# In the 128-row tiles of a mixture-of-experts FFN, layer 1 takes the high and low halves of the rows side by side, and VectorE adds the two halves of each PSUM bank

## The chip, the cores and the metric

The kernel runs on one core of one Trainium2 chip. Its time is the device time of one execution in microseconds (us). Three executions of the kernel before took 754.45, 755.43 and 755.51 us, so their median is 755.43 us. Besides these, one execution was recorded by the hardware profiler.

## The reference, cut to what matters

A block over x of shape (4, 1024, 256), that is 4096 tokens of 256 numbers. The first half is a gated linear recurrence with a residual. The second half is the mixture of experts that this change is about: each token goes to the two of eight experts that score highest.

```
x = x + ga * attn(layernorm(x) * (1 + ca) + sa)
h = layernorm(x) * (1 + cb) + sb
scores = softmax(h @ Wg + bg);  the two best experts of each token, weights normalised
for e in range(8):                       # W1[e]: 256 x 1024, W2[e]: 1024 x 256
    hid = gelu(h @ W1[e] + b1[e])
    y   = hid @ W2[e] + b2[e]
    output += y * combine_w[..., e]
x = x + gb * output
```

Everything is float32. The kernel reaches that accuracy with TensorE's faster fp32r format by splitting each operand a into a high part (a rounded to fp32r) and a low part (a minus the high part), and adding the products high x high, high x low and low x high.

## The kernel before, in words

**The dispatch.** In the first 300 us the recurrence runs over eight groups of 512 tokens. GpSimd (POOL) writes each token's row with indirect DMAs into the lists of its two experts in DRAM (`disp_x`, L530). The semaphores `sent0` and `sent1` count the rows that have landed, of groups 0 to 3 and 4 to 7.

**The experts.** Then each of the eight experts works through its list in tiles of 256 rows (`TE`): a first tile, a hardware loop over k further ones, and, where the rest of the list fits in 128 rows, one more tile of 128 rows behind a branch (`more_tiles`, L261; `parts` is 2 for a tile of 256 rows and 1 for one of 128). I call the last kind a half tile. All engines run the same list of tiles, each with its own instruction stream, and meet at semaphores.

**One tile.** The rows are loaded into `xin` a tile ahead (SyncE, L360), turned by TensorE into `tp` (L944), rounded by ScalarE into `fh` (L767) and subtracted by VectorE into `fl` (L1296). Layer 1 (`layer1`, L960) makes the hidden units in eight chunks f = 0 to 7 of 128 units; chunk f goes to PSUM bank `mm[f % 4]`, columns 0 to 255, as six matmuls of 256 columns (two halves k of the contraction, three products each). In a half tile the same 256 columns are computed, of which 128 are used. ScalarE then takes GELU twice from the bank, once rounded into `hh` (L783) and once in place (L784); VectorE subtracts the two into `hl` (L1330). Layer 2 (`layer2`, L969) multiplies `hh` and `hl` with W2, three matmuls of 256 columns for each f and each 128 rows.

**The order on TensorE.** layer 1 of f = 0 to 3; then for f = 4 to 7 layer 1 of f and layer 2 of f - 4; layer 2 of f = 4; the turn of the next tile's rows; layer 2 of f = 5 to 7. Since there are four banks, layer 1 of f = 4 waits until `hl` of f = 0 is made (`hidden_low`), and so on. The next tile's layer 1 waits for its `fl` (`rows_low`).

**The order on VectorE.** The eight subtractions `hl`, with small operations between them; `fl` of the next tile; a copy of the token columns; then the end of the tile, which waits for layer 2: bias (`ytmp`, L1350) and, for each 128 rows, the weighted result `ysb` (L1359), which waits until an earlier scatter from the same buffer has landed (`y_sent0`, `y_sent1`). POOL scatters `ysb` to the output with an added DMA (L576). So VectorE comes to `hl` of f = 0 of the next tile only when the last tile's `ysb` are written.

**Weights.** W1 and W2 of later experts are loaded by SyncE (1 MB each), and split into high and low parts between the operations of each expert's first tile.

Of the kernel before, what the change touches and what calls it, by code (L numbers as in the profile page):

```python
# [44 lines left out]
    "total_counted", "counts_ready", "gate_diff", "gate_sigmoid", "weights_ready", "pad_places", "pads_sent0",  # L45
    "pads_sent1", "few_ready", "pads_done", "meta_made", "meta_copied", "gb_loaded", "tick_pool", "tick_sp",
    "raw_loaded0", "raw_loaded1", "split_high1", "split_high2", "split_low1", "split_low2", "rows_loaded",
    "rows_turned", "rows_high", "rows_low", "layer1_done", "gelu_done", "hidden_low", "layer2_done", "y_taken",
    "y_ready", "y_sent0", "y_sent1", "dve_a", "dve_b", "dve_c", "act_own", "pool_own",
)  # L50

# [1 line left out]
def build(nc, x, rms, split, W_K, W_ugg, W_out, Wg, bg, W1, b1, W2, b2, c, wmod, out):  # L53
# [9 lines left out]
    with ExitStack() as ctx:  # L63
# [77 lines left out]
        with ExitStack() as p2:  # L141
            SH = [None, None]
            SL = [None, None]
            for i in range(2):
                SH[i] = sb(p2, f"SH{i}", [128, 4096], F32R)
                SL[i] = sb(p2, f"SL{i}", [128, 4096], F32R)
            xin = sb(p2, "xin", [128, 2, DW])
            xm = sb(p2, "xm", [128, 2, MW])
            tokb = sb(p2, "tokb", [128, 2], I32)
            wsl = sb(p2, "wsl", [128, 3, 2, 2])  # L150
            wB = sb(p2, "wB", [128, 2])
            nom = sb(p2, "nom", [128, 2])
            gbr = sb(p2, "gbr", [128, 2, D])
            fh = sb(p2, "fh", [128, 2, TE], F32R)
            fl = sb(p2, "fl", [128, 2, TE], F32R)
            hh = sb(p2, "hh", [128, NF, TE], F32R)
            hl = sb(p2, "hl", [128, NF, TE], F32R)
            ysb = sb(p2, "ysb", [128, 2, D])
            ytmp = sb(p2, "ytmp", [128, 2, D])
            tokn = sb(p2, "tokn", [128, 2], I32)  # L160
            b1T = sb(p2, "b1T", [128, E * NF])
# [128 lines left out]
        def sp_program(e):  # L290
# [68 lines left out]
                for j in range(2):  # L359
                    e.dma_start(xin[:, j, :], rows_of(j)).then_inc(S["rows_loaded"], 16)  # L360

            r_late, r_soon, r_sooner, r_sent = (e.alloc_register("sp_" + k) for k in ("late", "soon", "sooner", "sent"))
            e.wait_ge(S["late_ready"], 1)
            e.reg_load(r_late, lateint[0:1, 0:1])
            e.reg_load(r_soon, lateint[0:1, 1:2])
            e.reg_alu(r_soon, r_soon, 1, ALU.logical_shift_left)
            e.reg_add(r_sooner, r_soon, 1)
# [10 lines left out]
            for n in range(E):  # L378
                if n == 1:
                    e.wait_ge(S["pads_done"], 1)  # L380
                if n:
                    e.reg_load(r_last, nmint[0:1, n:n + 1])
                e.reg_mov(r_pos, 0)

                def rows_of(j):
                    e.reg_alu(r_at, r_pos, r_last, ALU.min)
                    e.reg_add(r_at, r_at, n * CAP)
                    e.reg_add(r_pos, r_pos, 128)
                    return Xd[bass.ds(e.snap(r_at, min_val=0, max_val=E * CAP - 128), 128), :]

                def wait_for_groups():

                    e.reg_add(r_sent, r_pos, TE)
                    e.reg_alu(r_sent, r_sent, 1, ALU.logical_shift_left)
                    e.reg_alu(r_sent, r_sent, r_soon, ALU.max)
                    e.reg_alu(r_sent, r_sent, r_sooner, ALU.min)
                    e.reg_alu(r_sent, r_sent, 1, ALU.bitwise_and)
                    e.reg_alu(r_sent, r_sent, 8, ALU.logical_shift_left)
                    e.reg_add(r_sent, r_sent, SENT_6)
                    e.reg_alu(r_sent, r_sent, SENT_6, ALU.max)  # L400
                    e.wait_ge(S["sent1"], r_sent)
                    e.sem_inc(S["tick_sp"], 1)

                def tile(first, parts):
                    if n == 0 and not first:
                        wait_for_groups()
                    load(rows_of)
                    if first and n == 0:
                        e.wait_ge(S["x2_scaled"], NG)
                        e.wait_ge(S["x2_scaled_last"], 1)  # L410
                        e.wait_ge(S["x2_stored0"], 16 * (NG // 2))
                        e.wait_ge(S["x2_stored1"], 16 * (NG // 2))
                        load_b2(0, 1)
                        e.wait_ge(S["counts_ready"], 2)
                        e.reg_load(r_last, nmint[0:1, n:n + 1])
                    if first and n + 2 < E:
                        split_done(e, n)
                        load_w1(n + 2)

                if n == 0:  # L420
                    tile(True, 2)
                    ks = counts_of(e)
                    more_tiles(e, ks, n, tile)
                    e.wait_ge(S["sent1"], SENT_8)
                    load_b2(1, E)
                else:
                    tiles(e, ks, n, tile)
                if n + 2 < E:
                    load_w2(n + 2)
# [187 lines left out]
            due("y_sent1", 0)  # L617

        def act_program(e):
            rl, due = counter(e, "act", ("layer1_done", "layer2_done", "rows_turned"))  # L620
# [155 lines left out]
            for n in range(E):  # L776
                def tile(first, parts):
                    c_ = slice(0, 128 * parts)
                    for f in range(NF):
                        due("layer1_done", 1)  # L780
                        due("layer2_done", 1)
                        bias = b1T[:, n * NF + f:n * NF + f + 1]
                        e.activation(hh[:, f, c_], mm[f % 4][:, c_], ACT.Gelu_apprx_tanh, bias=bias)  # L783
                        e.activation(mm[f % 4][:, c_], mm[f % 4][:, c_], ACT.Gelu_apprx_tanh, bias=bias)\  # L784
# [10 lines left out]
        def pe_program(e):  # L795
# [154 lines left out]
            for n in range(E):  # L950
# [9 lines left out]
                def layer1(f, parts):  # L960
                    if f >= 4:
                        due("hidden_low", 1)
                    for k in range(2):
                        for t, (a, b) in enumerate(((w1h, fh), (w1h, fl), (w1l, fh))):
                            i = e.matmul(mm[f % 4][:, 0:TE], a[:, k, f * 128:(f + 1) * 128], b[:, k, :],  # L965
# [31 lines left out]
                tiles(e, ks, n, tile)  # L997

        def dve_program(e):
            rl, due = counter(e, "dve", ("gelu_done", "rows_high", "layer2_done", "y_taken", "y_sent0", "y_sent1", "rows_loaded", "gb_loaded", "dve_c"))  # L1000
# [308 lines left out]
            for n in range(E):  # L1309
# [3 lines left out]
                def tile(first, parts):  # L1313
# [10 lines left out]
                    if first:  # L1324
                        mark(e.tensor_scalar(nom[:, :], nom0, float(n * CAP), None, ALU.add))
                        due("dve_c", 1)
                    for f in range(NF):
                        due("gelu_done", 1)
                        w_ = slice(0, 128 * parts)
                        e.tensor_tensor(hl[:, f, w_], mm[f % 4][:, w_], hh[:, f, w_].bitcast(F32), ALU.subtract)\  # L1330
                            .then_inc(S["hidden_low"], 1)
                        if f in small:
                            if f > 0:
# [73 lines left out]
```

## Time and profile before

| what | value |
|---|---|
| median of three executions | 755.43 us (754.45 to 755.51) |
| span of the profiled execution | 770.2 us |
| TensorE busy | 705.5 us (92%) |
| VectorE busy | 517.6 us (67%) |
| ScalarE busy | 416.1 us (54%) |
| mean granted TensorE clock | 0.956 |

The profiled execution has no other time than its span, 770.2 us; it is 14.8 us (2%) above the median of the others. The experts take from about 312 us to its end. A busy time of TensorE counts each matmul with its modelled end, which overlaps the next one: the pace is the distance between two starts. `MATMUL mm<-fh,SH` is a layer 1 product of high rows with high weights, `fl` and `SL` are the low parts. "issue" is a wait with no cause in the trace. In a row of the timeline the bracket at the end tells how long the engine sat idle before the instruction and what ended it.

### The profile page before, as it was taken

Reading aid. Unit: us, or ns where it says so; the run is one execution under the profiler, and the core shown is the slowest. Engines: PE = TensorE matmul, PEld = TensorE weight load, DVE = VectorE, ACT = ScalarE, POOL = GpSimd, SP = SyncE. Lnnn points to the kernel's source line nnn. Section 1 sums busy time; section 2 is a strip of 40 time slices with the busy share of each in tenths; the row PEclk is TensorE's granted clock in tenths of the full one; section 3 lists DMA queues with packets and bytes.
Section 4 is the critical chain, followed back from the end, with each engine's and each line's share of the span. In section 5 each row is a group of like instructions: output and inputs, shape, how many; then the busy total and the mean of one; then the engine's idle time right before and its main releaser. Section 6 shows DMA issues by size and latency. Waiting matters only on the chain.

```text
span 770.2 us, 16815 instructions
## 1 busy us (share of the span) xinstructions
PE 705.5 (92%) x4854; PEld 651.0 (85%) x4854; DVE 517.6 (67%) x1788; ACT 416.1 (54%) x1082; POOL 393.3 (51%) x309
## 2 busy tenths in 40 slices
PE   5899999999999993489998999999998999999991
PEld 1678888788888873389998999999898999999991
DVE  5878879998887668375553754647866476476451
ACT  5456564655546351165654755547665575475560
POOL 1264637785683654633534635446555445463443
PEclk9799999999999995589999999999999999999996
DMA  8441012230110413414457344555553553433432
GB/s 300 146 160 56 1 55 71 83 112 29 56 55 31 153 69 106 152 40 73 62 111 175 61 73 64 121 132 166 124 114 63 123 130 91 100 62 63 74 70 37
DMA packets 50308, 72.54 MB, mean 94 GB/s; under 512 B 5808, under 2 KB 42108, under 8 KB 50240
## 3 DMA queue, kind: packets, MB, share of 16 engines
q0 software_dynamic: 16480, 27.28, 19.4%
q1 hardware_dynamic: 33760, 44.46, 18.4%
q8 instruction: 29, 0.48, 0.3%
q14 instruction: 39, 0.32, 0.1%
HBM read 48.85 MB, written 22.87 MB: 93 GB/s over the span
## 4 chain that ended last, share of the span: by engine, by line
PE 76%; DVE 9%; issue 6%; DMA 4%; ACT 2%; POOL 2%; SPq 0%; DVEq 0%; another core or an unknown queue 0%; POOLq 0%; ACTq 0%
PE mm L965 24%; PE yb L976 23%; PE mm L810 17%; PE yb L835 5%; PE tp L944 2%; DMA out_x<-ysb,tokb 2%; PE tp L866 1%; PE tp L825 1%; PE tp L853 1%; DVE hl L1330 1%; ACT xnb L651 1%; DMA mb<-mod_rows 1%; DMA gbr<-mod_rows,xm 1%; DVE bst L1011 1%; DMA h2all<-in_L_wmod 1%
## 5 line engine op out<-in xcount | busy, mean ns | idle before, releaser
L783 ACT ACTIVATE hh<-mm,b1T 128x256 fp32r<-128x256 f32 (+1 forms) x288 | 135.9, 472 | 174.5 <-PE mm L965 124.5
L576 POOL DMA_INDIRECT out_x<-ysb,tokb x68 | 109.2, 1606 | 187.2 <-DVE ysb L1359 147.0
L1330 DVE TENSOR_TENSOR hl<-mm,hh 128x256 fp32r<-128x256 f32 (+1 forms) x288 | 116.3, 407 | 128.5 <-ACT mm L784 115.3
L965 PE MATMUL mm<-fh,SH 128*128 128x256 f32 x576 | 166.4, 289 | 22.7 <-DVE hl L1330 8.4
L965 PE MATMUL mm<-fl,SH 128*128 128x256 f32 x576 | 163.3, 283 | 0.0
L965 PE MATMUL mm<-fh,SL 128*128 128x256 f32 x576 | 162.9, 283 | 0.0
L976 PE MATMUL yb<-SH,hh 128*128 128x256 f32 x544 | 156.9, 288 | 0.0
L976 PE MATMUL yb<-SH,hl 128*128 128x256 f32 x544 | 153.6, 282 | 0.0
L976 PE MATMUL yb<-SL,hh 128*128 128x256 f32 x544 | 153.5, 282 | 0.0
L965 PEld LDWEIGHTS mm<-fh,SH 128*128 128x128 f32 x576 | 110.7, 192 | 26.5 <-DVE hl L1330 10.3
L784 ACT ACTIVATE mm<-mm,b1T 128x256 f32<-128x256 f32 (+1 forms) x288 | 127.5, 443 | 0.0
L965 PEld LDWEIGHTS mm<-fl,SH 128*128 128x128 f32 x576 | 110.7, 192 | 0.0
L965 PEld LDWEIGHTS mm<-fh,SL 128*128 128x128 f32 x576 | 110.7, 192 | 0.0
L810 PE MATMUL mm<-xh,WH 128*128 128x512 f32 x256 | 107.4, 419 | 1.5 <-DVE xl L1061 1.4
L976 PEld LDWEIGHTS yb<-SL,hh 128*128 128x128 f32 x544 | 103.5, 190 | 0.0
L976 PEld LDWEIGHTS yb<-SH,hh 128*128 128x128 f32 x544 | 103.4, 190 | 0.0
L976 PEld LDWEIGHTS yb<-SH,hl 128*128 128x128 f32 x544 | 103.4, 190 | 0.0
L810 PE MATMUL mm<-xh,WL 128*128 128x512 f32 x256 | 101.7, 397 | 0.0
L810 PE MATMUL mm<-xl,WH 128*128 128x512 f32 x256 | 101.0, 395 | 0.0
L571 POOL DMA_INDIRECT gbr<-mod_rows,xm x74 | 74.9, 1012 | 22.6 <-issue 22.2
L530 POOL DMA_INDIRECT disp_x<-h2all,pos x64 | 62.1, 971 | 29.4 <-issue 26.3
L835 PE MATMUL yb<-wog,og 128*128 128x256 f32 x256 | 60.3, 379 | 0.0
(218 smaller groups left out, 1172.8 us busy)
## 6 DMA issues: line engine op xcount, KB each, us to landing
xin<-disp_x SPq DMA_DIRECT2D x74, 132.0 KB
wraw<-in_L_ffn_W SPq DMA_DIRECT2D x8, 1024.0 KB
h2all<-in_L_ffn_W SPq DMA_DIRECT2D x8, 1024.0 KB
xb<-in_L_attn_x SPq DMA_DIRECT2D x8, 512.0 KB, 7.5
out_x<-x2b SPq DMA_DIRECT2D x8, 512.0 KB
mb<-mod_rows SPq DMA_DIRECT2D x3, 768.0 KB, 6.4
wraw<-in_L_attn_W_ugg SPq DMA_DIRECT2D x1, 1536.0 KB, 10.2
gbr<-mod_rows,xm POOLq DMA_INDIRECT x74
```

The source lines that it names most:

```text
L530: e.indirect_dma_start(out=Xd, out_offset=bass.IndirectOffsetOnAxis(ap=p[:, j:j + 1], axis=0), in_=h2all[:, j, :], in_offset=None).then_in ...
L571: e.indirect_dma_start(out=gbr[:, j, :], out_offset=None, in_=modd.rearrange("b (n d) -> (b n) d", d=D), in_offset=bass.IndirectOffsetOnAx ...
L576: e.indirect_dma_start(out=out_rows, out_offset=bass.IndirectOffsetOnAxis(ap=tokb[:, j:j + 1], axis=0), in_=ysb[:, j, :], in_offset=None, ...
L651: i = e.activation(xnb[:, j, :], hb[:, g % 4, j, :], ACT.Copy, scale=rin[:, g % 2, j:j + 1])
L783: e.activation(hh[:, f, c_], mm[f % 4][:, c_], ACT.Gelu_apprx_tanh, bias=bias)
L784: e.activation(mm[f % 4][:, c_], mm[f % 4][:, c_], ACT.Gelu_apprx_tanh, bias=bias)\
L810: i = e.matmul(mm[q][:, :], a[:, k, c0:c0 + 128], b[:, g % 2, k, :], start=(k == 0 and t == 0), stop=(k == 1 and t == 2))
L835: i = e.matmul(yb[j // 2][:, (j % 2) * D:(j % 2 + 1) * D], og[:, n % 2, j * 128:(j + 1) * 128], wog[:, (g // 2) % 2, hc, :], start=(hc == ...
L944: i = e.transpose(tp[k][:, j * 128:(j + 1) * 128], xin[:, j, k * 128:(k + 1) * 128], ident[:, :])
L965: i = e.matmul(mm[f % 4][:, 0:TE], a[:, k, f * 128:(f + 1) * 128], b[:, k, :], start=(k == 0 and t == 0), stop=(k == 1 and t == 2))
L976: i = e.matmul(yb[0][:, j * D:(j + 1) * D], a[:, f, j * 128:(j + 1) * 128], b[:, f, :], start=(f == 0 and j == 0 and t == 0), stop=(f == N ...
L1330: e.tensor_tensor(hl[:, f, w_], mm[f % 4][:, w_], hh[:, f, w_].bitcast(F32), ALU.subtract)\
```

## The change

Four things change. In a half tile, layer 1 of one f is four matmuls in place of six: the high and low rows (now the two planes of one tensor `fb`) stand side by side as 2 x 128 columns, once against the high and once against the low weights. The bank then holds two sums of 128 columns each. VectorE adds them with one TENSOR_REDUCE (`sum_half`) into columns 256 to 383 of the same bank, and a new semaphore `half_summed` tells ScalarE, which takes GELU from there. The product low x low is computed too. The order on VectorE in a half tile is: the sums of f = 0 and 1, then for each f the sum of f + 2 and the subtraction of f. In tiles of 256 rows VectorE and ScalarE keep their count of `layer1_done` or `half_summed` up with a register addition at most. Last, SyncE's rule for expert 0 changes: before, it worked out for each further tile whether the rows of groups 6 and 7 were needed (`wait_for_groups`); now it waits once for all groups (`SENT_8`) ahead of the second tile's load.

```diff
-            fh = sb(p2, "fh", [128, 2, TE], F32R)
-            fl = sb(p2, "fl", [128, 2, TE], F32R)
+            fb = sb(p2, "fb", [128, 2, 2, TE], F32R)
+            fh, fl = fb[:, 0, :, :], fb[:, 1, :, :]
...
                 def tile(first, parts):
-                    if n == 0 and not first:
-                        wait_for_groups()
                     load(rows_of)
...
                     tile(True, 2)
                     ks = counts_of(e)
+                    e.wait_ge(S["sent1"], SENT_8)
                     more_tiles(e, ks, n, tile)
-                    e.wait_ge(S["sent1"], SENT_8)
                     load_b2(1, E)
...  (ScalarE)
-                        due("layer1_done", 1)
+                        if parts == 1:
+                            e.reg_add(rl["layer1_done"], rl["layer1_done"], 1)
+                            due("half_summed", 1)
+                        else:
+                            due("layer1_done", 1)
...
+                        m_ = mm[f % 4][:, TE:TE + 128] if parts == 1 else mm[f % 4][:, 0:TE]
+                        e.activation(hh[:, f, c_], m_, ACT.Gelu_apprx_tanh, bias=bias)
+                        e.activation(m_, m_, ACT.Gelu_apprx_tanh, bias=bias)\
...  (TensorE, layer1)
+                    if parts == 1:
+                        for k in range(2):
+                            for t, a in enumerate((w1h, w1l)):
+                                i = e.matmul(mm[f % 4][:, 0:TE].rearrange("p (a t) -> p a t", a=2), a[:, k, f * 128:(f + 1) * 128],
+                                             fb[:, :, k, 0:128], start=(k == 0 and t == 0), stop=(k == 1 and t == 1))
+                        i.then_inc(S["layer1_done"], 1)
+                        return
...  (VectorE)
+                    def sum_half(f):
+                        due("layer1_done", 1)
+                        e.tensor_reduce(mm[f % 4][:, TE:TE + 128], mm[f % 4][:, 0:TE].rearrange("p (a t) -> p t a", a=2), AX, ALU.add)\
+                            .then_inc(S["half_summed"], 1)
+
+                    if parts == 1:
+                        sum_half(0)
+                        sum_half(1)
+                    else:
+                        e.reg_add(rl["layer1_done"], rl["layer1_done"], NF)
                     for f in range(NF):
+                        if parts == 1 and f + 2 < NF:
+                            sum_half(f + 2)
                         due("gelu_done", 1)
                         w_ = slice(0, 128 * parts)
-                        e.tensor_tensor(hl[:, f, w_], mm[f % 4][:, w_], hh[:, f, w_].bitcast(F32), ALU.subtract)\
+                        m_ = mm[f % 4][:, TE:TE + 128] if parts == 1 else mm[f % 4][:, 0:TE]
+                        e.tensor_tensor(hl[:, f, w_], m_, hh[:, f, w_].bitcast(F32), ALU.subtract)\
                             .then_inc(S["hidden_low"], 1)
```

VectorE, start of the half tile of expert 0, before (`mm0` to `mm3` are the banks):

```order
L1330 TENSOR_TENSOR hl<-mm0,hh 128x128
L1317 TENSOR_TENSOR wsl<-xm,nom 128x4
L279 REGISTER_ALU
L1330 TENSOR_TENSOR hl<-mm1,hh 128x128
L279 REGISTER_ALU
L1318 SCALAR_TENSOR_TENSOR wsl<-xm,wsl 128x4
L279 REGISTER_ALU
L1330 TENSOR_TENSOR hl<-mm2,hh 128x128
```

VectorE at the same place, with the change:

```order
L1323 TENSOR_REDUCE mm0<-mm0 128x128
L279 REGISTER_ALU
L1323 TENSOR_REDUCE mm1<-mm1 128x128
L279 REGISTER_ALU
L1323 TENSOR_REDUCE mm2<-mm2 128x128
L279 REGISTER_ALU
L1337 TENSOR_TENSOR hl<-mm0,hh 128x128
L1311 TENSOR_TENSOR wsl<-xm,nom 128x4
L279 REGISTER_ALU
L1323 TENSOR_REDUCE mm3<-mm3 128x128
L279 REGISTER_ALU
L1337 TENSOR_TENSOR hl<-mm1,hh 128x128
```

Three sums now stand ahead of the first subtraction, and one ahead of each later one.

TensorE, half tile of expert 0, layer 1 of f = 4 and layer 2 of f = 0, before:

```order
L279 REGISTER_ALU
L965 MATMUL mm0<-fh,SH0 128x256
L965 MATMUL mm0<-fl,SH0 128x256
L965 MATMUL mm0<-fh,SL0 128x256
L965 MATMUL mm0<-fh,SH0 128x256
L965 MATMUL mm0<-fl,SH0 128x256
L965 MATMUL mm0<-fh,SL0 128x256
L279 REGISTER_ALU
L976 MATMUL yb0<-SH0,hh 128x256
L976 MATMUL yb0<-SL0,hh 128x256
L976 MATMUL yb0<-SH0,hl 128x256
```

TensorE at the same place, with the change:

```order
L279 REGISTER_ALU
L953 MATMUL mm0<-fb,SH0 128x256
L953 MATMUL mm0<-fb,SL0 128x256
L953 MATMUL mm0<-fb,SH0 128x256
L953 MATMUL mm0<-fb,SL0 128x256
L279 REGISTER_ALU
L970 MATMUL yb0<-SH0,hh 128x256
L970 MATMUL yb0<-SL0,hh 128x256
L970 MATMUL yb0<-SH0,hl 128x256
```

Two of six layer 1 matmuls are gone from each f; nothing else on TensorE has moved.

## Rows read from the trace of the kernel before

**Rows 1.** The page: the chain that ended last, by engine.

```profile
PE 76%; DVE 9%; issue 6%; DMA 4%; ACT 2%; POOL 2%; SPq 0%; DVEq 0%; another core or an unknown queue 0%; POOLq 0%; ACTq 0%
```

**Rows 2.** Groups by shape: shapes, count, busy us, mean ns, idle before.

```profile
L783 ACT ACTIVATE hh<-mm,b1T 128x256 fp32r<-128x256 f32 x256 | 124.1, 485 | 152.3 <-PE mm L965 106.4 <-PE yb L976 18.0 <-issue 17.0
L783 ACT ACTIVATE hh<-mm,b1T 128x128 fp32r<-128x128 f32 x32 | 11.8, 367 | 22.2 <-PE mm L965 18.2 <-issue 1.7 <-PE yb L976 0.8
```

**Rows 3.** Timeline, third half tile (C): start us, us, engine, instruction.

```profile
616.40 0.28 PE L965 MATMUL mm<-fh,SH 128*128 128x256 f32 x1
618.59 0.28 DVE L1330 TENSOR_TENSOR hl<-mm,hh 128x128 fp32r<-128x128 f32 x1
623.35 0.37 ACT L783 ACTIVATE hh<-mm,b1T 128x128 fp32r<-128x128 f32 x1 [0.46 <-PE mm L965]
623.98 0.29 DVE L1330 TENSOR_TENSOR hl<-mm,hh 128x128 fp32r<-128x128 f32 x1 [0.77 <-ACT mm L784]
625.42 0.39 PE L965 MATMUL mm<-fh,SH 128*128 128x256 f32 x1
```

**Rows 4.** Groups by shape: the reduction and the scan nearest to the new operation.

```profile
L1074 DVE TENSOR_TENSOR_SCAN ob<-kb,mm 128x512 f32<-128x512 f32 x16 | 19.5, 1220 | 0.6
```

**Rows 5.** Timeline of VectorE around 314 us: a reduction.

```profile
314.57 0.39 DVE L1217 TENSOR_REDUCE kf<-ncmp 128x16 f32<-128x224 f32 x1
```

**Rows 6.** Timeline, first half tile (A).

```profile
410.67 0.28 PE L965 MATMUL mm<-fh,SH 128*128 128x256 f32 x1
414.97 0.15 DVE L1357 COPY tokb<-tokn 128x1 int32<-128x1 int32 x1 [2.61 <-DMA out_x<-ysb,tokb]
415.90 0.58 PE L965 MATMUL mm<-fh,SH 128*128 128x256 f32 x1 [2.27 <-DVE hl L1330]
419.05 0.34 PE L965 MATMUL mm<-fh,SL 128*128 128x256 f32 x1
422.01 0.37 ACT L783 ACTIVATE hh<-mm,b1T 128x128 fp32r<-128x128 f32 x1 [0.85 <-PE yb L976]
423.75 0.39 PE L965 MATMUL mm<-fh,SH 128*128 128x256 f32 x1
```

**Rows 7.** Timeline, second half tile (B).

```profile
506.43 0.28 PE L965 MATMUL mm<-fh,SH 128*128 128x256 f32 x1
513.69 0.37 ACT L783 ACTIVATE hh<-mm,b1T 128x128 fp32r<-128x128 f32 x1 [0.74 <-PE mm L965]
515.85 0.66 ACT L767 ACTIVATE fh<-tp 128x256 fp32r<-128x256 f32 x2 [1.57 <-PE tp L944]
517.08 0.39 PE L965 MATMUL mm<-fh,SH 128*128 128x256 f32 x1 [1.58 <-DVE fl L1296]
```

**Rows 8.** Timeline, fourth half tile (D).

```profile
661.45 0.28 PE L965 MATMUL mm<-fh,SH 128*128 128x256 f32 x1
669.10 0.37 ACT L783 ACTIVATE hh<-mm,b1T 128x128 fp32r<-128x128 f32 x1 [1.00 <-PE mm L965]
671.78 0.39 PE L965 MATMUL mm<-fh,SH 128*128 128x256 f32 x1 [1.09 <-DVE fl L1296]
```

**Rows 9.** Timeline, a full tile of expert 0: VectorE's first subtraction, TensorE's first layer 2.

```profile
401.15 0.42 DVE L1330 TENSOR_TENSOR hl<-mm,hh 128x256 fp32r<-128x256 f32 x1
401.50 0.15 DVE L1317 TENSOR_TENSOR wsl<-xm,nom 128x4 f32<-128x4 f32 x1
402.45 0.28 PE L976 MATMUL yb<-SH,hh 128*128 128x256 f32 x1
```

**Rows 10.** Timeline: the last dispatch, the second tile's load, its turn.

```profile
320.44 0.96 POOL L530 DMA_INDIRECT disp_x<-h2all,pos  x1 [0.30 <-issue]
327.62 1.11 SPq L360 DMA_DIRECT2D xin<-disp_x  x2
335.89 0.60 PE L944 MATMUL tp<-ident,xin 128*128 128x128 f32 x4
```

**Rows 11.** Timeline: a long wait of TensorE inside a full tile.

```profile
583.91 0.39 PE L965 MATMUL mm<-fh,SH 128*128 128x256 f32 x1 [2.32 <-DVE hl L1330]
```

More of the change, by code:

```diff
@@ L47 @@
     "raw_loaded0", "raw_loaded1", "split_high1", "split_high2", "split_low1", "split_low2", "rows_loaded",
-    "rows_turned", "rows_high", "rows_low", "layer1_done", "gelu_done", "hidden_low", "layer2_done", "y_taken",
+    "rows_turned", "rows_high", "rows_low", "layer1_done", "half_summed", "gelu_done", "hidden_low", "layer2_done", "y_taken",
     "y_ready", "y_sent0", "y_sent1", "dve_a", "dve_b", "dve_c", "act_own", "pool_own",
@@ L360, in load @@
                     e.dma_start(xin[:, j, :], rows_of(j)).then_inc(S["rows_loaded"], 16)
-            r_late, r_soon, r_sooner, r_sent = (e.alloc_register("sp_" + k) for k in ("late", "soon", "sooner", "sent"))
+            r_late = e.alloc_register("sp_late")
             e.wait_ge(S["late_ready"], 1)
             e.reg_load(r_late, lateint[0:1, 0:1])
-            e.reg_load(r_soon, lateint[0:1, 1:2])
-            e.reg_alu(r_soon, r_soon, 1, ALU.logical_shift_left)
-            e.reg_add(r_sooner, r_soon, 1)
             e.reg_mov(r_last, CAP - 128)
@@ L389, in rows_of @@
                     return Xd[bass.ds(e.snap(r_at, min_val=0, max_val=E * CAP - 128), 128), :]
[L391 to L402, printed above, removed]
                 def tile(first, parts):
-                    if n == 0 and not first:
-                        wait_for_groups()
                     load(rows_of)
@@ L619, in act_program @@
         def act_program(e):
-            rl, due = counter(e, "act", ("layer1_done", "layer2_done", "rows_turned"))
+            rl, due = counter(e, "act", ("layer1_done", "half_summed", "layer2_done", "rows_turned"))
             def weights_high(part, k):
@@ L779, in tile @@
                     for f in range(NF):
-                        due("layer1_done", 1)
+                        if parts == 1:
[3 more added lines that the diff above has]
+                            due("layer1_done", 1)
                         due("layer2_done", 1)
                         bias = b1T[:, n * NF + f:n * NF + f + 1]
-                        e.activation(hh[:, f, c_], mm[f % 4][:, c_], ACT.Gelu_apprx_tanh, bias=bias)
-                        e.activation(mm[f % 4][:, c_], mm[f % 4][:, c_], ACT.Gelu_apprx_tanh, bias=bias)\
+                        m_ = mm[f % 4][:, TE:TE + 128] if parts == 1 else mm[f % 4][:, 0:TE]
+                        e.activation(hh[:, f, c_], m_, ACT.Gelu_apprx_tanh, bias=bias)
+                        e.activation(m_, m_, ACT.Gelu_apprx_tanh, bias=bias)\
                             .then_inc(S["gelu_done"], 1)
@@ L999, in dve_program @@
         def dve_program(e):
-            rl, due = counter(e, "dve", ("gelu_done", "rows_high", "layer2_done", "y_taken", "y_sent0", "y_sent1", "rows_loaded", "gb_loaded", "dve_c"))
+            rl, due = counter(e, "dve", ("layer1_done", "gelu_done", "rows_high", "layer2_done", "y_taken", "y_sent0", "y_sent1", "rows_loaded", "gb_loaded", "dve_c"))
             def rsqrt(v, y, a):
```

## The prediction, made before the changed kernel ran

> **What bounds the kernel now.** I read the page first. The chain that ended last is 76% TensorE and 9% VectorE [rows 1], so a matmul less is worth its time only where TensorE doesn't wait anyway. Then I read the groups by shape, to see how much of the kernel the change reaches: ScalarE's GELU ran 256 times on 256 columns and 32 times on 128 [rows 2]. At eight per tile that is 32 full tiles and only 4 half tiles. Then the timeline of the four half tiles, which I call A, B, C and D, from the first matmul of layer 1 to the first one of the next tile: A 423.75 - 410.67 = 13.08 us [rows 6], B 517.08 - 506.43 = 10.65 [rows 7], C 625.42 - 616.40 = 9.02 [rows 3], D 671.78 - 661.45 = 10.33 [rows 8]. Together 43.1 us; all else is out of the change's reach but for small things named below.
>
> In C TensorE doesn't wait at all: 72 matmuls and a turn of about 0.56 us fill 9.02 us, so one matmul costs (9.02 - 0.56) / 72 = 0.1175 us at full clock. In A, VectorE waited 2.61 us for a scatter of the output to land, TensorE waited 2.27 us for VectorE's first `hl`, and came back at half its clock: 14 starts in 419.05 - 415.90 = 3.15 us [rows 6], 0.225 each with the first longer one. B and D end in a wait of 1.58 and 1.09 us for `fl` of the next tile [rows 7, 8].
>
> **What is removed.** 2 of 6 matmuls for each of 8 f in 4 tiles: 64 x 0.1175 = 7.5 us of TensorE's work. That is the most there is to win, 1%. Whether it is won depends on who is late instead, at two places of each half tile.
>
> **The head of a half tile.** Layer 1 of f = 4 needs `hl` of f = 0. In C VectorE is busy with the last tile until 618.59, 2.19 us after the tile's first matmul, and begins `hl` at once [rows 3]; it is done, and TensorE may go on, some 0.32 us later, at 2.51, while TensorE itself has work until 24 x 0.1175 = 2.82. So there is a cover of 0.3 us. With the change TensorE is ready at 16 x 0.1175 = 1.88, and VectorE must first sum.
>
> The sum's price isn't in the trace. It reads 256 elements per row and writes 128. The nearest rows: a reduction of 224 elements took 0.39 us [rows 5], which with 32 elements more at VectorE's pace is about 0.42; the `hl` of a full tile, also 256 elements, took 0.42 [rows 9] and the operation behind it started 0.35 after it (401.50 - 401.15), before it was done. From below, the subtraction of 128 elements took 0.28 [rows 3]; from above, the scan took 1.220 us for 512, 0.61 for 256 [rows 4]. I take 0.42 with a step of 0.34 to 0.35, since the reduction and the subtraction of that size agree. The Trainium skill ("VectorE: DVE Perf Modes", section "Rules for kernel authors") says of a reduction on a hot path to expect the 1x pace, calls it VectorE's slowest operation and advises to restructure. The trace bears out 1x, 0.39 us for 224, but not that it would be slower than a subtraction: by the row the sum stays at 0.42.
>
> So, counted from the tile's first matmul: sum 0 from 2.23 to 2.65; sums 1 and 2 behind it occupy VectorE until 3.25; GELU of f = 0 starts at 2.69, and from the start of that pair to the subtraction 0.63 us pass (623.35 to 623.98, [rows 3]), so 3.32; `hl` 0.29 more, 3.61; TensorE goes on at 3.65. Before, it went on at 2.82. The head costs TensorE 3.65 - 1.88 = 1.77 us of waiting, and 0.83 us net.
>
> **The middle.** From there to the end of layer 1 of f = 7 there are 16 layer 1 and 9 layer 2 matmuls, 25 x 0.1175 = 2.94, to 6.69 with the longer first one. `hl` of f waits behind sum f + 2 on VectorE, which waits for layer 1 of f + 2. I followed each f: sum 4 can start at 4.3 and `hl` of f = 2 is done at 4.9, needed at 5.3; later ones have 0.3 to 0.5 us to spare. It doesn't bind. Queued behind those waits on VectorE are only the small operations, which nobody waits for soon.
>
> **The tail.** Behind layer 1 of f = 7 come its GELU, then ScalarE's `fh` of the next tile, then VectorE's `fl`, and the next tile's first matmul waits for that. In A this took 423.75 - 422.01 = 1.74 us from the start of the last GELU [rows 6], and nothing else was in the way; in C 2.07, where the turn came later than the GELU. Before, the last GELU began 6.95 us (C), 7.26 (B) and 7.65 (D) into the tile [rows 3, 7, 8]. Now: last matmul at 6.85, sum 7 until 7.31, GELU at 7.35. TensorE's own work ends at about 8.9. With each tile's tail:
> - C: 7.35 + 1.74 = 9.09, before 9.02: +0.07.
> - B: its tail is 517.08 - 513.69 = 3.39 (ScalarE began `fh` only at 515.85, long after the turn); 7.35 + 3.39 = 10.74, before 10.65: +0.09.
> - D: tail 2.68; 10.03, before 10.33: -0.30.
> - A: TensorE is held by VectorE until 5.23. It is now held 1.46 us after VectorE comes free in place of 0.32, 1.14 us more, until 6.37. Then 25 matmuls, 14 of them at the slow pace again, 3.15 + 11 x 0.1175 = 4.44, to 10.81; then 0.16 + 0.46 + 0.04 to the GELU and 1.74: 13.21, before 13.08: +0.13.
>
> Sum: -0.01 us. The whole 7.5 us is given back, at the head because VectorE isn't free, at the tail because the last GELU comes no earlier.
>
> **The rest.** In full tiles VectorE gets one register addition ahead of the first `hl`. No row shows one alone; it is surely under the 0.15 us of a whole one-element copy [rows 6]. There `hl` is done at 401.15 + 0.42 = 401.57, and layer 1 of f = 4 starts at 402.45 - 6 x 0.1175 = 401.74 [rows 9]: a cover of 0.17, so nothing; with the cover gone at most 32 x 0.15 = 4.8 us. SyncE's earlier wait for all groups: the last dispatch was issued by 321.4, while the second tile's load went out at 327.62 and is turned at 335.89 [rows 10]. Those 6.2 us ahead of the load are room enough for the last rows to land, and another 8.3 us lie between the load and the turn: nothing; each us beyond both would cost one. The matmul itself reads two pieces of 128 columns in place of 256 in one; I expect 0.1175 for it too; were it double, 128 more such steps, 15 us, but each piece is still read in order.
>
> So the forecast is no change: the profiled span stays at 770.2, and the median, 2% below it, at 755.4.
>
> **The rivals.**
> 1. TensorE-bound: VectorE hides the sums after all. For it speaks the chain's 76% TensorE; against it the head above, which even with sums of 0.28 us starts f = 4 no earlier than 2.23 + 0.28 + 0.04 + 0.63 + 0.29 + 0.04 = 3.51. 755.4 - 7.5 = 747.9.
> 2. The unexplained lateness of `fh` at the end of B and D goes (3.39 and 2.68 against 1.74, so 1.65 + 0.94 = 2.6 us). ScalarE sat idle 1.57 us there after the turn [rows 7] with no cause shown. The Trainium skill ("Runtime: NRT & Kernel Launch", section "Instruction fetch mechanics") says that a taken branch to code outside the fetched pages waits for a DMA; the half tile's end is next to such a branch, and the trace agrees in so far as the wait has no other cause. The change moves every later instruction, so such a wait may go, or come where there was none. Gone from B and D: 752.8. Come to A and C as in B: 755.4 + 3.3 = 758.7.
> 3. Slower: the clock falls. The change makes TensorE idle for 1.8 us at the head of B, C and D, where it didn't wait. After 2.27 us of waiting in A it came back at half clock [rows 6], after 2.32 us elsewhere it didn't [rows 11], so 1.8 is near where it may. Each fall costs 3.15 - 14 x 0.1175 = 1.5 us: one, 756.9; all three, 759.9. It decides if the granted clock drops in those tiles.
> 4. Slower: the sum costs as the scan, 0.61. Three sums ahead of the first `hl` and the last one ahead of the last GELU: 4 x 0.27 = 1.1 us per tile, 4.3 in all, 759.7.
>
> **How the numbers follow.** The forecast has 0.45, rival 1 0.03, rival 2 gone 0.19 and come 0.07, rival 3 0.15, rival 4 0.08, and 0.03 is left for a dearer matmul. About 0.2% (1.5 us) is what a measurement of this kernel can tell from no change. Faster is 0.03 + 0.19 = 0.22, the same 0.45, slower 0.33. The range leaves out rival 1 and the far ends of 3 and 4: 752.5 to 759.0. The likeliest case's own range is 753.9 to 756.9.
>
> **What would show it.** Right: 1.5 to 2 us of idle TensorE before layer 1 of f = 4 in B, C and D, ended by VectorE's `hl`, three reductions of about 0.42 us ahead of it, and half tiles of nearly the same length as before, C near 9.1. Wrong: C near 7.1 us (rival 1); a last GELU well before 7.35 or an `fh` that starts at once in B and D (rival 2); matmul starts 0.21 apart after the head (rival 3); reductions of 0.6 us (rival 4); or the second tile's load later than the turn needs it.

## The result, and the profile after

| kernel | median | executions |
|---|---|---|
| before | 755.43 us | 5, 754.03 to 756.07 |
| with the change | 760.23 us | 5, 757.68 to 762.20 |

The ratio is 1.0067, with a 95% interval of 1.0043 to 1.0092: the change costs about 5 us, where I had forecast none, and the time lies outside my range. The profiled execution of the changed kernel took 762.2 us with a span of 760.5, so what lies around the span is 1.7 us.

I read the chain that ended last first, since it answers to [rows 1]:

```profile
PE 74%; DVE 8%; DMA 6%; issue 5%; POOL 3%; ACT 2%; SPq 0%; DVEq 0%; POOLq 0%; ACTq 0%
```

DMA has gone from 4% to 6%. Most of that is the scatter `out_x<-ysb,tokb`, 22.0 us of the chain against 12.4; but kernels without the loss come to 22 us of it too (e5 and e6 below). New in the chain are 2.4 us of the last dispatch and 2.9 us of the load of `xin`, in expert 0. What that load holds up shows in the groups by shape (shapes, count, busy us, mean ns, idle time before and its releasers): first the turn of the next tile's rows, then the new matmul of the half tiles, the sum, and ScalarE's GELU of 128 columns, the last answering to [rows 2].

```profile
L931 PE MATMUL tp<-ident,xin 128*128 128x128 f32 x148 | 23.2, 281 | 6.5 <-DMA xin<-disp_x 6.5
L953 PE MATMUL mm<-fb,SH 128*128 128x256 f32 x64 | 17.7, 305 | 8.5 <-DVE hl L1337 8.5
L1323 DVE TENSOR_REDUCE mm<-mm 128x128 f32<-128x256 f32 x32 | 13.0, 428 | 4.5 <-PE mm L953 3.7
L770 ACT ACTIVATE hh<-mm,b1T 128x128 fp32r<-128x128 f32 x32 | 12.0, 374 | 24.5 <-DVE mm L1323 24.4
```

The sum takes 0.428 us. TensorE waits 8.5 us in all for VectorE at the head of the four half tiles, and, once, 6.5 us for rows of `xin`. The second is the surprise, and the timeline places it in expert 0. POOL's last dispatch and its gather, SyncE's load of the second tile, and the turn of those rows on TensorE (start us, us, engine, instruction), where [rows 10] stood:

```profile
318.20 0.96 POOL L512 DMA_INDIRECT disp_x<-h2all,pos  x1 [0.30 <-issue]
319.46 0.98 POOL L553 DMA_INDIRECT gbr<-mod_rows,xm  x1 [0.30 <-issue]
...
322.07 7.54 SPq L360 DMA_DIRECT2D xin<-disp_x  x4
...
325.65 1.11 PE L931 MATMUL tp<-ident,xin 128*128 128x128 f32 x4 [6.52 <-DMA xin<-disp_x]
```

The load goes out 2.9 us after the last dispatch left POOL (318.20 + 0.96 = 319.16), as soon as all rows have landed; the rows are turned 3.6 us later, and TensorE stands idle for 6.52 us. In [rows 10] the load lay 6.2 us behind the last dispatch and the turn another 8.3 us behind it, with no wait.

The half tiles, on the other hand, did what was forecast. TensorE and VectorE in half tile C, which answers to [rows 3]: the first matmul, the three sums, the first `hl`, the return of TensorE, the last GELU:

```profile
607.23 0.28 PE L953 MATMUL mm<-fb,SH 128*128 128x256 f32 x1
...
609.42 1.09 DVE L1323 TENSOR_REDUCE mm<-mm 128x128 f32<-128x256 f32 x3
610.59 0.29 DVE L1337 TENSOR_TENSOR hl<-mm,hh 128x128 fp32r<-128x128 f32 x1
...
610.93 0.39 PE L953 MATMUL mm<-fb,SH 128*128 128x256 f32 x1 [1.66 <-DVE hl L1337]
...
614.73 0.37 ACT L770 ACTIVATE hh<-mm,b1T 128x128 fp32r<-128x128 f32 x1 [0.22 <-DVE mm L1323]
```

Counted from the first matmul: VectorE free at 2.19, `hl` at 3.36, TensorE back at 3.70 after 1.66 us of waiting, last GELU at 7.50, next tile at 9.25. I had forecast 2.19, 3.32, 3.65, 1.77, 7.35 and 9.09.

### The profile page after: what moved, and what is told of

The parts are those of the page before. It is cut to its first block, busy times and chain, and to the rows that moved or that the text cites. A ratio compares the mean times of both kernels' runs of the same rounds, so it can differ in the third digit from the quotient of the medians.

```text
span 760.5 us, 16723 instructions
## 1 busy us (share of the span) xinstructions
PE 698.4 (92%) x4790; PEld 644.1 (85%) x4790; DVE 527.3 (69%) x1820; ACT 416.8 (55%) x1082; POOL 394.5 (52%) x309
## 4 chain that ended last, share of the span: by engine, by line
PE 74%; DVE 8%; DMA 6%; issue 5%; POOL 3%; ACT 2%; SPq 0%; DVEq 0%; POOLq 0%; ACTq 0%
PE yb L970 22%; PE mm L959 19%; PE mm L797 19%; PE yb L822 6%; DMA out_x<-ysb,tokb 3%; PE tp L931 2%; POOL disp_x L512 1%; PE tp L853 1%; PE tp L812 1%; DMA gbr<-mod_rows,xm 1%; DVE ytmp L1357 1%; PE tp L840 1%; PE mm L953 1%; DMA mb<-mod_rows 1%; DMA h2all<-in_L_wmod 1%
## 5 line engine op out<-in xcount | busy, mean ns | idle before, releaser
L959 PE MATMUL mm<-fb,SH 128*128 128x256 f32 x1024 | 191.4, 285 | 8.0 <-DVE hl L1337 5.6
L959 PEld LDWEIGHTS mm<-fb,SH 128*128 128x128 f32 x1024 | 158.5, 191 | 11.0 <-DVE hl L1337 7.0
L959 PE MATMUL mm<-fb,SL 128*128 128x256 f32 x512 | 144.3, 282 | 0.0
L959 PEld LDWEIGHTS mm<-fb,SL 128*128 128x128 f32 x512 | 97.7, 191 | 0.0
L797 PEld LDWEIGHTS mm<-xh,WH 128*128 128x128 f32 x256 | 48.9, 191 | 11.9 <-DVE xl L1055 1.8
L797 PEld LDWEIGHTS mm<-xh,WL 128*128 128x128 f32 x256 | 48.7, 190 | 11.0
## 6 DMA issues: line engine op xcount, KB each, us to landing
wraw<-in_L_attn_W_ugg SPq DMA_DIRECT2D x1, 1536.0 KB, 10.1
```

The source lines that it names most:

```text
L797: i = e.matmul(mm[q][:, :], a[:, k, c0:c0 + 128], b[:, g % 2, k, :], start=(k == 0 and t == 0), stop=(k == 1 and t == 2))
```

## The experiments

The base of the experiments is the kernel before with the last step of SyncE's rule written another way (e1). All runs below but e3 and e5 keep SyncE's old rule, and they have this branch too. Times of one row are compared through their ratio to the kernel before on the same chip. "First two" is the length of expert 0's first two tiles from the first layer 1 matmul, A to D are the half tiles, all from one profiled execution of each kernel:

| run | ratio to before | median us | span | first two | A | B | C | D |
|---|---|---|---|---|---|---|---|---|
| e1_before_branch | 0.9999 (0.9983 to 1.0015) | 754.58 | 752.2 | 32.36 | 9.84 | 9.03 | 9.02 | 9.18 |
| e2_half_only | 0.9998 (0.9979 to 1.0016) | 754.54 | 753.9 | 32.36 | 12.76 | 9.25 | 9.23 | 9.29 |
| e3_wait_only | 1.0066 (1.0043 to 1.0090) | 759.82 | 758.5 | 35.27 | 11.39 | 9.02 | 9.02 | 9.19 |
| e4_128_columns | 1.0005 (0.9977 to 1.0032) | 755.14 | 751.2 | 31.37 | 9.40 | 8.79 | 8.79 | 9.08 |
| e5_wait_later | 0.9996 (0.9976 to 1.0015) | 755.41 | 754.6 | 31.58 | 12.98 | 9.23 | 9.25 | 9.27 |
| e6_early_gather | 0.9960 (0.9942 to 0.9979) | 751.54 | 751.6 | 29.03 | 12.70 | 9.05 | 9.05 | 9.19 |
| e7_no_sum | 0.9987 (0.9972 to 1.0001) | 753.66 | 750.9 | 31.39 | 8.70 | 7.94 | 7.94 | 8.26 |
| e8_sum_twice | 1.0099 (1.0074 to 1.0125) | 762.78 | 761.4 | 31.54 | 13.11 | 12.01 | 10.91 | 12.02 |
| e9_gather_and_128 | 0.9984 (0.9962 to 1.0007) | 752.37 | 753.4 | 29.03 | 13.56 | 8.79 | 8.78 | 9.07 |
| e10_gather_and_half | 0.9962 (0.9945 to 0.9978) | 752.39 | 751.3 | 30.50 | 11.97 | 9.23 | 9.22 | 9.28 |
| with the change | 1.0067 (1.0043 to 1.0092) | 760.23 | 760.5 | 35.08 | 13.53 | 9.23 | 9.25 | 9.28 |

**e1_before_branch.** The kernel before, its wait on a computed number turned into a branch:

```diff
-                    e.reg_alu(r_sent, r_sent, 8, ALU.logical_shift_left)
-                    e.reg_add(r_sent, r_sent, SENT_6)
-                    e.reg_alu(r_sent, r_sent, SENT_6, ALU.max)
-                    e.wait_ge(S["sent1"], r_sent)
+                    with e.If_ne(r_sent, 0):
+                        e.wait_ge(S["sent1"], SENT_8)
```

> The kernel before, with SyncE's rule for expert 0 kept but its last step written as a branch around a constant wait for all groups, in place of a wait on a computed value. It is the base of the other runs and gives a second profile. Theory W (the single early wait for all groups is what made the changed kernel slower) and theory H (the half tiles did) both expect 755.4 us within 1.5. Both also expect a span near 753.7, since the runs' times lie 1.7 us above the span where both are known, and no wait of TensorE for the second tile's rows. If instead the first tile here also waits some 7 us for code or rows, the profiled 770.2 us of the kernel before was usual, and W loses its ground.

It takes as long as before, so it can stand in for it. Its span is 752.2 us, 18 us less than that of the execution whose trace I had predicted from. SyncE's queue, the last dispatch on POOL, and TensorE's turn and first wait in the second tile:

```profile
313.70 26.04 SPq L360 DMA_DIRECT2D xin<-disp_x  x6
...
318.19 0.96 POOL L528 DMA_INDIRECT disp_x<-h2all,pos  x1 [0.30 <-issue]
...
318.81 0.60 PE L942 MATMUL tp<-ident,xin 128*128 128x128 f32 x4
327.95 0.58 PE L963 MATMUL mm<-fh,SH 128*128 128x256 f32 x1 [3.61 <-DVE hl L1328]
```

In this execution the second tile's load goes out at 313.70, **before** the last dispatch, not after it: those rows come from earlier groups. The turn at 318.81 waits for nothing. Half tiles B and D are 9.03 and 9.18 us long, not 10.65 and 10.33 as in [rows 7, 8].

**e2_half_only and e3_wait_only.** The two parts of the change apart. e2 has its half tiles and SyncE's old rule; e3 has the old half tiles and the new rule:

```diff
-                def wait_for_groups():
...
-                    if n == 0 and not first:
-                        wait_for_groups()
...
                     ks = counts_of(e)
+                    e.wait_ge(S["sent1"], SENT_8)
                     more_tiles(e, ks, n, tile)
-                    e.wait_ge(S["sent1"], SENT_8)
```

> The changed kernel with the old rule of SyncE put back (as a branch): the half tiles' change alone. Theory W: 755.4 within 1.5, half tiles B, C, D at 9.2 to 9.3 us and the turn of the second tile on time. Theory H: about 760, as the changed kernel (760.2).

> The kernel before with SyncE waiting once for all groups ahead of the second tile's load: the wait alone, half tiles as before. Theory W: 759 to 762, with TensorE idle for about 6.5 us ahead of the second tile's turn, less what it would have waited for later anyway. Theory H: 755.4 within 1.5.

e3 alone gives the whole change in time, 1.0066 against 1.0067, and e2 gives none, 0.9998. The profile of e3 shows the same rows as the changed kernel:

```profile
318.41 0.96 POOL L512 DMA_INDIRECT disp_x<-h2all,pos  x1 [0.30 <-issue]
...
323.27 19.60 SPq L360 DMA_DIRECT2D xin<-disp_x  x6
...
326.34 1.11 PE L926 MATMUL tp<-ident,xin 128*128 128x128 f32 x4 [7.08 <-DMA xin<-disp_x]
```

TensorE waits 7.08 us, but the first two tiles are only 2.9 us longer than in e1 (35.27 against 32.36), since the 3.61 us that e1's second tile waits for `hl` are gone: one wait has taken in the other. The spans differ by 6.3 us. Another 1.55 us lie in A, and 2.25 in a full tile of 15.85 us at 565.76 against 13.60, whose only wait is this one. TensorE comes back at full clock, and 1.4 us later 15 matmuls start 0.21 us apart:

```profile
571.04 0.39 PE L947 MATMUL mm<-fh,SH 128*128 128x256 f32 x1 [2.32 <-DVE hl L1312]
```

Whether these two belong to the earlier wait or to that one execution, the runs don't settle; in the other eleven profiled executions the same full tile took 11.8 to 14.3 us.

**e5_wait_later.** The changed kernel, with the wait moved behind the second tile's load:

```diff
                     ks = counts_of(e)
+                    k, half = count_of(e, ks, n)
+                    tile(False, 2)
                     e.wait_ge(S["sent1"], SENT_8)
-                    more_tiles(e, ks, n, tile)
+                    with e.Fori(1, k):
+                        tile(False, 2)
+                    with e.If_ne(half, 0):
+                        tile(False, 1)
```

> The changed kernel with its single wait for all groups moved one load down: behind the load of expert 0's second tile, ahead of the third tile's. Theory W says that the wait costs because the second tile's rows are needed at 319 us, before the last dispatch has landed, and the third tile's only at about 336: 754.5 us within 1.5, no wait ahead of the second tile's turn. A rival W2, that it isn't the place of the wait but SyncE's changed code, expects 760 as before.

0.9996: the loss is gone with everything else of the change in place. The load goes out at 313.08, and TensorE's first wait in the second tile is again VectorE's:

```profile
313.08 25.84 SPq L360 DMA_DIRECT2D xin<-disp_x  x6
...
327.90 0.51 PE L964 MATMUL mm<-fb,SH 128*128 128x256 f32 x2 [4.18 <-DVE hl L1342]
```

**e4_128_columns.** e1, with layer 1 of half tiles on the 128 columns that are used:

```diff
-                            i = e.matmul(mm[f % 4][:, 0:TE], a[:, k, f * 128:(f + 1) * 128], b[:, k, :],
+                            i = e.matmul(mm[f % 4][:, 0:128 * parts], a[:, k, f * 128:(f + 1) * 128], b[:, k, 0:128 * parts],
```

> The base with the six layer 1 matmuls of a half tile on 128 columns in place of 256, and nothing summed: another way to drop the wasted half. If a matmul's cost goes by its columns (about 0.06 us), layer 1 of a half tile falls from 5.6 to 2.8 us; TensorE then waits for VectorE's first hl until 2.5 us, and the tile takes about 7.4 us in place of 9.0: 6 us less in all, 749. If 128 columns cost as the weights' load (0.19 us busy) or more, a half tile takes at least 12 us: 10 us more or worse.

Half the columns, and hardly faster, so neither of the two expected times came: starts lie 0.11 us apart in place of 0.1175.

```profile
598.68 0.27 PE L963 MATMUL mm<-fl,SH 128*128 128x128 f32 x1
598.79 0.28 PE L963 MATMUL mm<-fh,SL 128*128 128x128 f32 x1
598.90 0.27 PE L963 MATMUL mm<-fh,SH 128*128 128x128 f32 x1
599.01 0.28 PE L963 MATMUL mm<-fl,SH 128*128 128x128 f32 x1
```

So between 128 and 256 columns, with new weights for each matmul, the price goes by the count of matmuls far more than by their columns; that much the change got right in dropping two of six.

**e7_no_sum.** e2 without the sums: ScalarE and VectorE read columns 0 to 127 of the bank, so the products with the low half of the rows are left out of the half tiles' results. The matmuls stay.

```diff
-                        if parts == 1:
-                            e.reg_add(rl["layer1_done"], rl["layer1_done"], 1)
-                            due("half_summed", 1)
-                        else:
-                            due("layer1_done", 1)
+                        due("layer1_done", 1)
...
-                        m_ = mm[f % 4][:, TE:TE + 128] if parts == 1 else mm[f % 4][:, 0:TE]
+                        m_ = mm[f % 4][:, 0:128 * parts]
...
-                    if parts == 1:
-                        sum_half(0)
-                        sum_half(1)
...
-                        if parts == 1 and f + 2 < NF:
-                            sum_half(f + 2)
```

> The half tiles' change alone (with the old rule of SyncE) and without VectorE's sums: ScalarE and VectorE read columns 0 to 127, so the products with the rows' low half are left out of the result in the half tiles. What the sums cost. Theory of the prediction: TensorE goes on with f = 4 at 2.5 us into the tile in place of 3.7, the tile takes 7.9 us in place of 9.25: 1.35 us each in B, C and D, 4 to 5 us in all with A, 750. Rival, that the half tile is bound by its tail (last GELU, fh, fl) whatever the sums do: 9 us and 754.5.

Free of the sums, the half tiles fall to 32.84 us together, from 37.07 in e1, 4.2 less. The half tile is as long as expected, but the time isn't: of those 4.2 us some 0.9 show (0.9987 against 0.9999, intervals that overlap), because the full tiles right behind them grow from 49.37 us (11.90, 12.79, 12.77, 11.91) to 52.82 (13.13, 13.59, 13.27, 12.83). VectorE at the end of C, and TensorE's wait in the tile after it:

```profile
608.57 0.17 DVE L1307 COPY xm<-xin 128x16 f32<-128x16 f32 x1 [2.30 <-DMA gbr<-mod_rows,xm]
608.68 0.42 DVE L1357 TENSOR_TENSOR ytmp<-yb,x2b 128x256 f32<-128x256 f32 x1
...
610.58 0.50 PE L971 MATMUL mm<-fb,SH 128*128 128x256 f32 x2 [1.19 <-DVE hl L1337]
```

`gbr` is gathered by POOL, which does so only behind the last tile's scatters; a tile shorter than POOL's round waits for it. In e2 it is the reverse: those four tiles take 48.07 us, 1.3 less than in e1, so the next tile also takes back part of a loss.

**e8_sum_twice.** e2 with each sum issued a second time into unused columns of the bank:

```diff
                         due("layer1_done", 1)
+                        e.tensor_reduce(mm[f % 4][:, TE + 128:TE + 256], mm[f % 4][:, 0:TE].rearrange("p (a t) -> p t a", a=2), AX, ALU.add)
```

> The half tiles' change alone (old rule of SyncE), each sum made twice, the first time into columns 384 to 511, which nobody reads. Theory: VectorE's sums lie on the path at the head (three more steps of 0.34 us, or four with the first one) and at the tail (one): 1.4 us more for each half tile, 10.6 in B, C and D, 5 to 6 us in all, 760. Rival, that the sums are hidden and the half tile waits for something else: 754.5.

The half tiles take 48.05 us, 7.5 more than in e2, and the time follows (1.0099 against 0.9998, 7.6 us). The head of B, VectorE's last repeated sum and first `hl`, then TensorE:

```profile
496.40 0.42 DVE L1339 TENSOR_REDUCE mm<-mm 128x128 f32<-128x256 f32 x1
496.73 0.42 DVE L1340 TENSOR_REDUCE mm<-mm 128x128 f32<-128x256 f32 x1
497.06 0.28 DVE L1354 TENSOR_TENSOR hl<-mm,hh 128x128 fp32r<-128x128 f32 x1
...
497.39 0.38 PE L969 MATMUL mm<-fb,SH 128*128 128x256 f32 x1 [2.46 <-DVE hl L1354]
...
498.66 0.41 PE L969 MATMUL mm<-fb,SH 128*128 128x256 f32 x1
498.87 0.42 PE L969 MATMUL mm<-fb,SL 128*128 128x256 f32 x1
499.08 0.42 PE L986 MATMUL yb<-SH,hh 128*128 128x256 f32 x1
```

Six sums step by 0.33 us and push the first `hl` of a half tile 0.8 us back, from 3.36 us after the first matmul to 4.18. C, 10.91 long, shows the sums alone, 1.7 us above e2. In B and D the matmuls start 0.21 apart for a while, and each costs a further 1.1 us, which I had not expected. The table by stretch shows the granted clock there (the column before "DMA share": stretch, its length, busy time and count of PE, PEld, DVE, ACT and POOL, clock, DMA share, GB/s), in B and then in C: half, the 1.2 GHz level, against full.

```profile
498.70:502.00 3.30, 3.30 (x18) 3.30 (x17) 2.61 (x11) 1.59 (x7) 2.58 (x3) 0.50 0.57 95
609.50:614.00 4.50, 4.50 (x36) 4.21 (x35) 4.50 (x21) 2.84 (x11) 3.48 (x3) 1.00 0.71 93
```

The clock fell after 2.46 us of idle TensorE in B and D and held after 2.49 us in C.

**e6_early_gather.** Since e1's second tile waits 3.61 us for `hl`, and `hl` for VectorE, which waits 3.82 us for `gbr`, I moved POOL's first gather ahead of the last group's eight dispatches:

```diff
-            send(g, 0)
-            send(g, 1)
-
-            e.wait_ge(S["counts_ready"], 2)
-            ks = counts_of(e)
...
+            e.reg_mov(rl["meta_copied"], 1)
+            gather()
+            send(g, 0)
+            send(g, 1)
+
+            e.wait_ge(S["counts_ready"], 2)
+            ks = counts_of(e)
...
-            e.reg_mov(rl["meta_copied"], 1)
-            gather()
```

> Not about the change but about what hides behind its wait. Base: the kernel before with the branch. There the second tile waits 3.6 us for VectorE, which waits 3.8 us for the first gather of gb rows, queued on POOL behind the last dispatches. Here POOL issues that gather ahead of the last group's eight dispatches. Theory: the second tile's wait and its half clock go, 3.6 us and up to 1.5 more: 750 us within 1.5, and the last rows land 2.6 us later without harm. Rival: the third tile's load or POOL's own later work takes the wait over, and it stays at 754.5.

751.54 us, 0.9960: faster than both kernels, though a little less than the 750 expected. First e1, then e6, on VectorE:

```profile
324.87 0.63 DVE L1299 COPY xm<-xin 128x16 f32<-128x16 f32 x1 [3.82 <-DMA gbr<-mod_rows,xm]
```

```profile
320.58 0.16 DVE L1300 COPY xm<-xin 128x16 f32<-128x16 f32 x1
...
322.52 3.28 DVE L1358 SCALAR_TENSOR_TENSOR ysb<-ytmp,wB,gbr 128x256 f32<-128x256 f32 x1
```

The wait for `gbr` is gone, and the second tile is 14.57 us long in place of 17.94. What comes next stands in the second row: one `ysb`, 0.48 us elsewhere, takes 3.28, all but its end while POOL runs the row below, and TensorE still waits 2.55 us.

```profile
321.73 3.77 POOL L240 TENSOR_TENSOR SL<-h2all,SH 128x512 fp32r<-128x512 f32 x3
```

The twelve profiled executions have 68 `ysb` each. Only five of all took over 0.7 us, and all five ran beside these POOL operations: one each in e6, e9 and e10 (3.28, 3.04 and 3.10 us), and two in the kernel before (1.36 and 1.32). No run takes the POOL operations away, so the cause is argued from this, not shown.

**e9_gather_and_128 and e10_gather_and_half.** The early gather with e4's edit, and with e2's half tiles.

> The early gather (751.5 us, 0.4% faster) with the half tiles' layer 1 and rows cut to 128 columns (755.1, no change by itself). Theory: a matmul of 128 columns starts every 0.112 us in place of 0.1175 only, so four half tiles give 4 x 48 x 0.0055 = 1.1 us at most, and what they give is partly taken back by the gather of the next tile; so 750.5 to 751.5. If the two changes hide each other, 751.5 or above; if fewer columns were worth half a matmul's time (the rival: the price of a matmul goes by its columns), 192 x 0.06 = 11 us less, 740.

> The early gather with the change's half tiles (four matmuls and a sum per f), SyncE's rule as before. Theory: half tiles are worth nothing on average (0.9998 by themselves), so the ratio is that of the early gather, 0.996, 751.5 us. If shorter tiles on TensorE had been held back by the gather in the second tile only, less: 750. Half tile A is to keep its idle time of over 3 us ahead of f = 4 and its slow matmuls, while C stays at 9.2.

752.37 and 752.39 us. Neither beats the early gather alone. The half tiles are worth nothing on this base too. e9's interval (0.9962 to 1.0007) overlaps e6's (0.9942 to 0.9979) and also takes in no gain at all, so it says only that no gain from 128 columns is seen. Half tile A of e10 keeps its slow matmuls, after 2.88 us of idle TensorE where I had expected over 3.

## Why the prediction was wrong

**The step that failed** is "SyncE's earlier wait for all groups: [...] nothing". I had read it from [rows 10]: load at 327.62, 6.2 us after the last dispatch. That the last rows land within 6.2 us was right; they took 2.9. What failed was to take the order of these two rows as the kernel's own. In the profiled execution the load came 14 us later than in e1 (327.62 against 313.70), when the last dispatch was long out. In e1, whose time is that of the kernel before, the load is 4.5 us ahead of the last dispatch and the wait would have held it. I had the warning in hand: the span of the profiled execution was 14.8 us above the median of the times, although a time also holds the 1.7 us around its span, so like for like it was 16.5 us longer. I noted the gap and priced all terms in the longer execution. Its first two tiles began 5.3 us later than e1's (312.24 against 306.95) and took 351.79 - 312.24 = 39.55 us, 7.2 more, so the third began 12.5 us later. ScalarE, VectorE and TensorE there:

```profile
323.46 0.47 ACT L783 ACTIVATE hh<-mm,b1T 128x256 fp32r<-128x256 f32 x1 [10.08 <-remote]
324.31 0.42 DVE L1330 TENSOR_TENSOR hl<-mm,hh 128x256 fp32r<-128x256 f32 x1 [7.74 <-ACT mm L784]
324.79 0.58 PE L965 MATMUL mm<-fh,SH 128*128 128x256 f32 x1 [7.44 <-issue]
```

ScalarE stood still first, with no cause in the trace; VectorE's `hl` waited for it, and TensorE started 0.06 us after that `hl` was done. The late load has a stall of its own. Six of SyncE's register instructions between its read of the tile counts and the load (L255 to L263) took 0.7 to 1.4 us each, where in e1 they took 0.03 to 0.05. One of them, L259, in the kernel before and then in e1 (count, shortest, median and longest ns, first and last start):

```profile
L259 SPq MOVE  x1: 1387/1387/1387, 324.0 to 324.0; - x1
```

```profile
L259 SPq MOVE  x1: 37/37/37, 312.5 to 312.5; - x1
```

From VectorE's last value for these counts (`kpk`, 315.59 and 310.14) to the load it was 12.0 us against 3.6. So 8.5 of the 13.9 us were SyncE's own delay and 5.4 came before it. What made ScalarE and SyncE slow in this one execution stays open.

What the wait costs: 5.1 us by the times (e3 against e1: 1.0066 - 0.9999, of 755). Of it 2.7 to 3.9 us lie in the first two tiles, which took 35.08 and 35.27 us in the two kernels with the earlier wait, and 31.37 to 32.36 in the six with the old order of load, dispatch and gather (e1, e2, e4, e5, e7, e8). The third tile began 2.7 to 4.5 us later than in those six. From there to the end the two took 418.4 and 416.0 us, and the eight runs without the earlier wait, e8 apart, 412.3 to 417.3, so single profiled executions can't place the rest. One number may point to the clock: over the timed executions the mean granted clock was 0.962 to 0.964 in e3 and 0.964 to 0.972 in e1. The rest is open.

**The half tiles** were right in mechanism and nearly in size, in B, C and D. That they gain nothing was forecast; that the total is off comes from the wait alone.
- The sum: 0.42 forecast, 0.428 measured; step 0.34, measured 0.33 to 0.34 (e8). Rival 4 (as the scan, 0.61) falls. The Trainium skill ("VectorE: DVE Perf Modes", section "Rules for kernel authors") calls a reduction VectorE's slowest operation; its 1x pace agrees with the trace, but the subtraction of the same 256 elements took 0.421 us in the changed kernel, so here a reduction is hardly slower.
- The head: 1.77 us of waiting forecast, 1.66 to 1.68 measured in B, C and D. Rival 1 (TensorE-bound, C near 7.1 us) falls: even without the sums (e7) C takes 7.94 us, and most of such a gain goes back to the next tile.
- The matmul from two pieces: 0.1175 forecast, and 0.118 between starts in the changed kernel.
- Lengths: C 9.09 forecast, 9.25 measured. B and D were forecast at 10.74 and 10.03 and took 9.23 and 9.28, but they took 9.03 and 9.18 in e1 already. The lateness of `fh` there was again of that one execution. Against e1, the three are longer by 0.20, 0.23 and 0.10 us.
- A was under-priced. VectorE's wait for the scatter varies, so TensorE's idle time there was 0.39, 0.51, 1.54, 1.84, 2.07 and 2.27 us in six executions of the old half tile, and 2.88 to 3.88 in four of the new one. The three sums add to it, and in all four the clock is half for 16 to 25 matmuls there. The head of A in the changed kernel, beside [rows 6], and the granted clock there and in C:

```profile
404.32 0.15 DVE L1364 COPY tokb<-tokn 128x1 int32<-128x1 int32 x1 [1.69 <-DMA out_x<-ysb,tokb]
...
406.46 0.58 PE L953 MATMUL mm<-fb,SH 128*128 128x256 f32 x1 [3.46 <-DVE hl L1337]
406.84 0.41 PE L953 MATMUL mm<-fb,SL 128*128 128x256 f32 x1
407.05 0.42 PE L953 MATMUL mm<-fb,SH 128*128 128x256 f32 x1
```

```profile
407.00:411.00 4.00, 4.00 (x21) 4.00 (x20) 1.74 (x9) 1.82 (x7) 3.16 (x3) 0.50 0.73 87
608.00:616.00 8.00, 6.34 (x54) 6.14 (x54) 6.99 (x28) 5.11 (x18) 4.55 (x4) 1.00 0.77 202
```

In e2 the half tiles take 40.53 us against 37.07 in e1, 3.5 more, 2.9 of them in A. The tiles behind them give back 1.3, and e1's A was one of the two short ones; the times show no difference at all. So "the whole gain is given back" stands: four sets of 16 matmuls, 7.5 us, bought nothing.

**Rival 2** (a late `fh` that goes or comes) had 0.26 of my chance. In every execution profiled since, B and D are as long as C to within 0.35 us (e8 apart, where the clock fell), so as far as these executions tell, there was nothing of it in the timed kernel that could go. I had connected it with the Trainium skill's rule on fetching behind a taken branch ("Runtime: NRT & Kernel Launch", section "Instruction fetch mechanics"). No run here shows or excludes that this was what stood still, there or in SyncE and ScalarE in expert 0.

**Rival 3** (the clock falls) didn't come true in B, C and D: after 1.65 to 1.68 us of idle TensorE the clock held, in twelve half tiles of four kernels (changed, e2, e5, e10). It did come in A, and in two of e8's.

## What to carry to other kernels

Compare the span of the profiled execution with the timed ones before reading an order of events from it: where it is longer by more than what lies around a span, find the stretch that is longer, and read no slack from that stretch. A wait that is made coarser (all rows in place of the rows needed) has to be priced against the earliest time at which the waiting transfer can go out, not the one seen. And work taken off TensorE in a short tile is worth nothing where VectorE isn't free at its head, or where the next tile's gather follows a round of its own.

## What was not expected of the hardware

- A matmul with fresh weights costs nearly the same for 128 columns as for 256, 0.11 us against 0.1175 from start to start (e4).
- A VectorE operation of 0.48 us took 3.28 while GpSimd ran elementwise work of 3.77 us beside it (e6), and 3.04 and 3.10 in e9 and e10.
- The length of one idle stretch doesn't decide whether TensorE's clock falls. It held after 1.65 to 1.68 us (twelve times), 2.07 (A of e3), 2.32 [rows 11] and 2.49 (C of e8), and fell after 1.54 (A of e9), 1.84 (A of e6), 2.27 [rows 6], 2.32 (e3) and 2.46 (B and D of e8). In A of e6 TensorE first came back at full clock, at 399.65, and the fall came 1.0 us later:

```profile
399.60:400.60 1.00, 0.95 (x8) 0.95 (x9) 0.93 (x7) 0.00 (x0) 1.00 (x1) 1.00 0.84 344
400.80:403.00 2.20, 2.20 (x12) 2.20 (x12) 0.36 (x2) 0.97 (x4) 1.59 (x3) 0.50 0.54 61
```

- In one of the twelve profiled executions ScalarE stood still for 10.1 us with no cause in the trace, and register instructions of SyncE took 0.7 to 1.4 us in place of 0.04, so that its next load came 8.5 us late by that alone.
